# Two node-update ticks behind the last group of each edge stage, instead of ticks ahead of it

## Time and profile before

| | us |
|---|---|
| three runs | 2838.57, 2837.82, 2832.29 (median 2837.82) |
| the profiled execution's own time | 2831.61 |
| span of its trace | 2829.6 |

### The profile page before, as it was taken

How to read it: one execution, slowest core, us unless ns; L and a number is a source line. 1 busy time by engine, 2 the same in 40 slices (tenths; PEclk the granted TensorE clock), 3 DMA queues, 4 the chain that set the end, 5 groups by cost and what they waited for, 6 DMA issues and landing times.

```text
span 2829.6 us, 25622 instructions
## 1 busy us (share of the span) xinstructions
PE 1862.6 (66%) x6464; PEld 875.8 (31%) x6464; DVE 1963.3 (69%) x3488; ACT 1101.4 (39%) x2157; POOL 1862.3 (66%) x1775
## 2 busy tenths in 40 slices
PE   1688778761888567777588856677488868882000
PEld 0333333320344233332244423333244434431000
DVE  4777777743777658999699959999599959972000
ACT  0112121120566435444366625555366636650000
POOL 0777777765775075552677756564577757777776
PEclk7889898975899879999799979999799979995555
DMA  0222222221455434332344434444334434442000
GB/s 15 57 64 64 64 77 64 64 63 44 146 176 176 158 100 136 107 109 95 89 120 128 120 90 146 153 146 149 104 121 125 123 101 140 144 131 63 23 21 20
DMA packets 228924, 285.58 MB, mean 101 GB/s; under 512 B 85309, under 2 KB 100697, under 8 KB 228652
## 3 DMA queue, kind: packets, MB, share of 16 engines
q1 hardware_dynamic: 172332, 257.60, 28.7%
q0 software_dynamic: 56448, 26.34, 5.2%
HBM read 173.01 MB, written 136.00 MB: 109 GB/s over the span
## 4 chain that ended last, share of the span: by engine, by line
DVE 28%; PE 16%; issue 13%; POOL 11%; ACT 6%; DMA 1%; DVEq 0%; SPq 0%; ACTq 0%; POOLq 0%
POOL out_dram L1705 7%; PE bank L1004 6%; DVE mn_total L1400 5%; DVE node_h L1208 5%; POOL mn_ring L447 4%; DVE node_h L1253 2%; PE bank L1756 2%; ACT node_square L1129 2%; DVE node_x L1232 2%; DVE mn_mean L1422 2%; DVE mn_cent L1424 2%; DVE mn_h L1480 2%; PE bank L1008 2%; PE bank L1013 2%; PE bank L998 2%
## 5 line engine op out<-in xcount | busy, mean ns | idle before, releaser
L447 POOL DMA_INDIRECT mn_ring<-slot_rows,addr_i x980 | 1042.4, 1064 | 620.6 <-issue 286.1
L1004 PE MATMUL bank<-node_x,center 128*128 128x512 f32 x492 | 258.4, 640 | 101.9 <-DVE node_h L1208 97.7
L447 POOL DMA_INDIRECT fr_xin<-in_x_dram,src_i x196 | 210.2, 1073 | 125.2 <-issue 125.2
L1008 PE MATMUL bank<-node_square,mean 128*128 128x512 f32 x492 | 263.3, 618 | 35.9 <-ACT node_std L1108 35.9
L447 POOL DMA_INDIRECT found<-node_table,look_i x196 | 210.7, 1075 | 89.1 <-issue 69.1
L1013 PE MATMUL bank<-node_h,wconv 128*128 128x512 f32 x492 | 267.0, 626 | 0.0
L447 POOL DMA_INDIRECT fr_xin<-in_x_dram,dst_i x196 | 204.2, 1042 | 59.7 <-issue 59.7
L595 PE MATMUL bank<-fr_s_lo,fr_s_hi 128*128 128x392 f16 x392 | 149.2, 381 | 138.0 <-DVE fr_d_lo L714 136.7
L1705 POOL DMA_INDIRECT out_dram<-keep,scat_i x196 | 192.6, 983 | 62.4 <-issue 62.4
L1018 PE MATMUL bank<-node_act,wconv 128*128 128x512 f32 x442 | 232.3, 608 | 1.2 <-ACT node_act L1123 1.2
L1123 ACT ACTIVATE node_act<-bank,bias 128x512 f32<-128x512 f32 x246 | 167.9, 682 | 126.1 <-PE bank L1013 125.8
(11 more groups left out here) (320 smaller groups left out, 3857.2 us busy)
## 6 DMA issues: line engine op xcount, KB each, us to landing
mn_ring<-local SPq DMA_DIRECT2D x120, 256.0 KB, 4.3
node_x_in<-in_x_dram SPq DMA_DIRECT2D x98, 256.0 KB, 3.0
out_dram<-node_rows SPq DMA_DIRECT2D x98, 256.0 KB, 3.3
mn_rin<-res SPq DMA_DIRECT2D x96, 256.0 KB, 3.3
local<-node_rows SPq DMA_DIRECT2D x96, 256.0 KB, 2.5
slot_rows<-keep SPq DMA_DIRECT2D x96, 256.0 KB, 2.0
mn_fcol<-f_rows SPq DMA_DIRECT2D x192, 128.0 KB, 4.1
res<-mn_x SPq DMA_DIRECT2D x72, 256.0 KB, 2.5
```

The lines of the kernel that those rows point to most:

```text
L447: return eng.indirect_dma_start(out=dest, out_offset=None, in_=table, in_offset=bass.IndirectOffsetOnAxis(ap=index, axis=0), bounds_check= ...
L1004: pe.matmul(bank[i][:, :], C["center"][:, :], src, start=True, stop=True).then_inc(s["centered"][i], 1)
L1008: pe.matmul(bank[4][:, :], C["mean"][:, :], nd.square[:, i - 1, :], start=True, stop=True) \
```

## The change

The ticks are dealt out anew, and the two that fall to a stage's last group come behind everything that this group has to do. `GAP` gives two ticks to the last group of A to E. `QUIET` leaves none to the groups ahead of it (the test is `g < GROUPS - 3`, so groups 22 and 23). The share of B and D falls from 0.83 to 0.72, since the same 130 ticks must be dealt out.

The diff, with each engine's loop in turn (VectorE, SyncE, TensorE, ScalarE):

```diff
-SHARE = dict(A=1.0, B=0.83, C=1.0, D=0.83, E=1.0, F=1.05)
+SHARE = dict(A=1.0, B=0.72, C=1.0, D=0.72, E=1.0, F=1.05)
+GAP = dict(A=2, B=2, C=2, D=2, E=2, F=0)
+QUIET = dict(A=3, B=3, C=3, D=3, E=3, F=4)
...
-        if g < GROUPS - 2 and (st != "F" or g < GROUPS - 4):
+        if g == GROUPS - 1:
+            due += GAP[st]
+        elif g < GROUPS - QUIET[st]:
             due += SHARE[st]
...
-                    for t in ticks[i][:1]:
-                        head(t)
+                    if g < n - 1:
+                        for t in ticks[i][:1]:
+                            head(t)
...
                     for t in ticks[i]:
-                        if t > ticks[i][0]:
+                        if g == n - 1 or t > ticks[i][0]:
                             head(t)
                         tail(t)
...
-                    for t in ticks[i]:
-                        keep_local(t)
+                    if g < n - 1:
+                        for t in ticks[i]:
+                            keep_local(t)
...
-                    for t in ticks[i]:
-                        tick(t)
+                    if g < n - 1:
+                        for t in ticks[i]:
+                            tick(t)
...
                         store(st, g)
                         if i + 1 < len(order):
                             fill_kv(*order[i + 1])
+                        for t in ticks[i]:
+                            keep_local(t)
+                            tick(t)
...
-                    for t in ticks[i][:1]:
-                        first(t)
+                    if g < n - 1:
+                        for t in ticks[i][:1]:
+                            first(t)
                     if st != "A":
                         product(i, st, g)
+                    if g == n - 1:
+                        back(i, st, g)
                     for t in ticks[i]:
-                        if t > ticks[i][0]:
+                        if g == n - 1 or t > ticks[i][0]:
                             first(t)
                         second(t)
-                    if g == n - 1:
-                        back(i, st, g)
...
-                    for t in ticks[i][:1]:
-                        begin(t)
+                    if g < n - 1:
+                        for t in ticks[i][:1]:
+                            begin(t)
...
-                    for t in ticks[i]:
-                        if t > ticks[i][0]:
-                            begin(t)
-                        rest(t)
                     if st in NORMS and g == n - 1:
                         squares(norm_at(st, g), g)
                         deviation(norm_at(st, g), g)
+                    for t in ticks[i]:
+                        if g == n - 1 or t > ticks[i][0]:
+                            begin(t)
+                        rest(t)
```

## The result

The changed kernel takes **2762.14 us** (median of 4 runs, 2761.4 to 2764.15); the kernel before, in its runs together with a repeat, 2835.07 (4 runs, 2832.29 to 2838.57). The ratio is 0.9743, with a 95% interval of 0.9726 to 0.976. The forecast was 2782, its range 2764 to 2808. The direction and the main mechanism held; the gain was larger than the sum, and the time lies just under the range. The profiled execution took 2762.42 us, its span 2760.5, at a mean granted clock of 0.867 (before: 0.856).

A forecast was written before the change was run, and what follows sets the result against it. No single engine bounds it: VectorE paces steps with ticks, GpSimd is the second limit and sets F's end. Terms summed to -55.4 from 2831.6, giving 2776.2; with 6.2 added, 2782; own range 2770 to 2796, over the cases 2764 to 2808.

The forecast's parts named there:

- C and E: Last steps of stages C and E: group 22 loses its tick, saving 5.2 us in each, -10.4 together.
- The pair: Two ticks behind a stage's last group: 19.9 us, hidden in VectorE's wait for gathers; +3 for overruns at B, C, E.
- R1: Stage ends: TensorE stays at half clock through the pair, 9 us at four or five boundaries; 2822, half 2800; chance 0.09.
- D's start: Start of D: ticks fall on groups 0 and 1, not 1 and 2, so scan 3 comes earlier; -5 us.
- R2: Tickless steps of B, D or E: GpSimd bounds them at 10.9 us, about 18 us in all; 2800; chance 0.08.
- R3: Stage boundaries: next stage's first gather goes behind the pairs, five of 19.9 us in the open; 2877, slower; chance 0.02.
- R5: Stage starts: each gather beside a tick takes twice its 0.99 us, 16 us at five boundaries; 2862, slower; chance 0.01.
- B's term, "-27.4": Steps of B: four ticks fewer at 7.48 us, 29.9, less 1.25 each for groups 22 and 23 at half clock.
- The overrun and the delay at B's start, +1.85: Start of B: +1 us for the pair sticking out, 0.85 for the first two groups' gathers beside a busy VectorE.
- A, "-2.0": End of A: one tick leaves the steps, 2.9 us saved, less 0.9 for a cold step.
- F, "+3.0" and the 0.85: Stage F: two-tick step moved to group 6 delays GpSimd's ring buffers, +3, bounds 0 to +8.5; delayed first gathers, 0.85.
- R4: Cold steps cost nothing, the pair ends early, stage starts run warm: 10 us better, 2772; chance 0.08.

The follow-up runs named there:

- the kernel without quiet steps: Changed kernel with ticks also in groups 22 and 23 of A, C and E, six fewer in B and D; 2756.36 us, ratio 0.9738.
- the run with the double back at 16: Changed kernel with F's step of two ticks moved from group 6 back to group 16; 2768.85 us, ratio 0.9753.

## Why the prediction came out 20 us high

**What held.** The chain of reasons: the gap takes two ticks, and the ticks that leave steps with a full price pay. Windows of the changed kernel, in order: steps 22 and 23 of A; step 6 of B, which has a tick; steps 21 to 23 of B; steps 22 and 23 of C; steps 22 and 23 of E (columns: length, busy of PE, PEld, DVE, ACT, POOL, clock, DMA):

```profile
953.24:962.33 9.09, 6.10 (x24) 3.05 (x24) 5.93 (x10) 3.35 (x7) 0.00 (x0) 0.86 0.23 69
962.33:968.96 6.63, 1.09 (x4) 0.72 (x4) 5.56 (x9) 1.14 (x3) 0.00 (x0) 0.50 0.47 159
...
1079.08:1094.53 15.45, 11.43 (x42) 5.32 (x40) 12.85 (x19) 8.60 (x19) 8.48 (x9) 1.00 0.45 144
...
1280.89:1288.91 8.02, 3.69 (x11) 1.96 (x12) 7.18 (x12) 1.62 (x4) 4.03 (x4) 0.70 0.02 4
1288.91:1296.86 7.95, 6.01 (x14) 2.56 (x13) 7.11 (x11) 1.62 (x4) 0.00 (x0) 0.50 0.40 132
1296.86:1304.82 7.96, 6.02 (x13) 2.34 (x11) 6.86 (x12) 1.62 (x4) 0.00 (x0) 0.50 0.38 132
...
1588.15:1593.32 5.17, 2.25 (x8) 1.45 (x9) 3.16 (x5) 0.69 (x1) 4.26 (x4) 0.81 0.38 110
1593.32:1599.02 5.70, 3.59 (x10) 1.64 (x9) 2.90 (x4) 0.69 (x1) 0.20 (x1) 0.50 0.39 124
...
2207.37:2213.49 6.12, 3.20 (x8) 1.66 (x9) 3.25 (x5) 0.69 (x1) 3.94 (x4) 0.64 0.43 122
2213.49:2219.19 5.70, 3.58 (x10) 1.64 (x9) 2.90 (x4) 0.69 (x1) 0.00 (x0) 0.50 0.33 98
```

*C and E.* Step 22 was forecast at 5.2 and is 5.17 in C; step 23 was to be 0.9 longer than 4.74, for a cold PE (one at half clock), and is 5.70 in both. In E step 22 is 6.12, with the clock at 0.64 already. The repeat of the same kernel had the clock in the same two steps of E:

```profile
2211.73:2216.45 4.72, 1.79 (x8) 1.00 (x9) 3.17 (x6) 0.69 (x1) 3.81 (x4) 1.00 0.36 102
2216.45:2221.20 4.75, 2.22 (x10) 1.18 (x9) 2.90 (x4) 0.69 (x1) 0.66 (x1) 0.85 0.46 137
```

So the cost of a cold PE in a step that VectorE doesn't fill is real, 9.47 against 11.82 us for the two, and whether it is paid varies from run to run.

*The pair* was forecast at 19.9 us, with 8.5 between its ticks, and is 19.3 with 8.45 at the end of E. At the ends of B and D it takes 16.1 and 16.3 us, and at A's end, with local ticks, 17.3 where 22 to 24 were forecast. TensorE's timeline at the end of E, as the earlier trace rows, shows that the clock comes back inside the first tick:

```profile
2223.21 1.91 PE L1013 MATMUL bank<-node_h,wconv 128*128 128x512 f32 x2
2224.92 1.66 PE L1008 MATMUL bank<-node_square,mean 128*128 128x512 f32 x2
...
2226.85 1.02 PE L1013 MATMUL bank<-node_h,wconv 128*128 128x512 f32 x2
```

That refutes R1. *D's start* was to gain 5; its scan 3 comes 54.66 us behind the first gather, before 59.90 (1707.54 - 1647.64). R2 didn't show in B or D: their tickless steps take 7.4 to 8.0 us, not 10.9. R3 is refuted by the first gathers, and by the pair moved to step 23, which is what an unhidden pair looks like. R5: eight gathers beside the pair took 10.66 us at F (2226.27 to 2236.93) and 11.13 to 11.37 at C, D and E; beside an idle VectorE they take 10.10. The prediction got "twice as long" from the lock on the Trainium skill's page "SBUF — State Buffer", section "SBUF: two separate sides". It left out a condition of that page: on VectorE's side the lock is for operations in a two-port mode, and for operations with two SBUF inputs only against a GpSimd operation that reads SBUF. Which of the pair's operations are of these kinds no run here shows. What was measured is 6 to 13%, and R5 is refuted for this mix of operations.

Three of the prediction's signs didn't come as written. The second waits are 3.2 to 5.2 us and not 1 to 3. C and E are shorter by 2.9 and 3.0 and not by 5; the prediction's own terms for them add up to 3.4. And the second L1013 row of the first tick, not of the second, is at 1.02 already.

**The step that failed is the size of B's term, "-27.4".** B fell by 33.6, the forecast with its additions was 25.5: 8.1 us of the 13.7 by which the sum fell short. Three parts:

- *"22 and 23 meet PE at half clock ...: 1.25 us each."* They take 7.95 and 7.96 at a granted clock of 0.50, and 7.95 was the price at 0.79. PE has 6.0 us of work in them, DVE 7: DVE still sets the pace and the slow products hide behind it. This part is 2.5 us. It was wrong to carry the 0.9 over from E, where DVE has only 2.9 and nothing hides them. The same error made D's term 1.3 too small.
- *"15.43"* as the step that goes. On average a step with a tick was dearer than that in the kernel before. Two windows of the kernel before, steps 7 and 9 of B:

```profile
1100.10:1117.51 17.41, 13.66 (x40) 6.62 (x39) 12.94 (x20) 8.81 (x19) 11.37 (x11) 0.81 0.40 127
1132.94:1149.22 16.28, 12.48 (x33) 4.97 (x32) 14.26 (x22) 7.68 (x16) 9.19 (x10) 0.90 0.34 109
```

  DVE is busy for 13 to 14 us of each, and PE works at a granted clock of 0.81 and 0.90. Step 6 of B, ahead of a tickless one, takes 15.45 in the changed kernel, at 1.00. 17.41 + 16.28 - 2 x 15.43 = 2.8 us. This part is luck as far as is known: it stands on one trace of the kernel before, and single steps of 16.4 to 16.5 us at a clock of 0.82 to 0.90 turn up early in B in other kernels of this set too, as steps 4, 6 and 8 of the kernel without quiet steps.
- *The overrun and the delay at B's start, +1.85.* Scan 3 comes 58.3 us behind the first gather, before 59.1: 0.8 us earlier instead of 1.85 later. This part is 2.7 us. The pair delays scan 0 by 5.6 us, but step 0 then takes 6.76 instead of 10.69, and step 1, which took 20.64 us at a clock of 0.78 (first line, the kernel before), takes 16.94 at 0.88 (second, the changed one):

```profile
1009.80:1030.44 20.64, 15.89 (x48) 7.78 (x47) 9.80 (x14) 8.61 (x17) 16.07 (x16) 0.78 0.27 82
1006.95:1023.89 16.94, 14.06 (x48) 6.80 (x47) 9.78 (x15) 8.61 (x17) 12.98 (x14) 0.88 0.31 89
```

*A, "-2.0"*, was -4.6. Its step 23 was priced 0.9 up for a cold PE, and instead falls from 9.09 to 6.63. VectorE waited there for PE in the kernel before:

```profile
967.96 0.69 DVE L1441 SCALAR_TENSOR_TENSOR mn_x<-bank,mn_rin 128x512 f32<-128x512 f32 x1 [2.36 <-PE bank L1772]
```

The same operation in the changed kernel:

```profile
963.52 0.67 DVE L1446 SCALAR_TENSOR_TENSOR mn_x<-bank,mn_rin 128x512 f32<-128x512 f32 x1
```

The wait has gone. A reading, not tried by itself: behind a step with a tick, PE is still at that tick's products when the turn is wanted (4.62 us of PE work in that window, 1.09 in the changed one). The window of before showed 9.09 for a step that follows one with a tick, and I took it for the price of any tickless step; the changed kernel's step 22, which does follow one, takes 9.09 still.

*F, "+3.0" and the 0.85*, was +0.6. Scan 7 was late and group 10 starts 109.3 us behind the first gather (before 107.7), so POOL does lose something: its ring waits in F are 6.7 us in six, the longest 2.1. But the wait of 3.94 at the end goes for it. The bound 0, "all of it eaten by that wait", was the right end, and the run with the double back at 16 confirms that the place of the double decides nothing. Together the misses of A, B, D and F are 15.2 us; C and E came out 0.9 us dearer, C by the later gather of D and E by its step 22, and the parts around the stages 0.6. That leaves 13.7.

**The offset of 6.2.** The median of the three first runs was 6.2 us above the profiled run, and I added it. The changed kernel's profile is 0.3 from its median. The 6.2 was a draw of chance: the untouched part ahead of the main phase took between 697.6 and 706.7 us in the ten profiles that are not from the slow chip, and a median of three carries such a spread. 13.7 + 6.2 = 19.9, the whole error. R4 named cold steps that cost nothing, a pair that ends early and warm stage starts. That held in part: cold steps cost nothing in A, B and D but did in C and E; the pairs at the ends of A, B and D ended early; and B's start ran warmer. Its size (10 us) and its chance (0.08) were too small, and the range's lower end rested on it.

What stays open: why scan 3 of B comes 0.8 us earlier where those of C and E come 1.3 and 0.8 later (C's 0.2 earlier in the repeat), and what varies in the untouched front phase. Neither was tried.

## What to carry to other kernels

Price a piece of filler work in each place by itself: here a tick costs mostly 7 to 8 us where VectorE sets the pace, 5 at the end of a stage that GpSimd feeds, 0.7 to 1.0 in its middle, and about nothing in the wait between two stages, up to the length of that wait. Before putting a price on a half clock, ask which engine ends last in that step; a cost seen in one stage is not to be carried to another with a different pace-setter. And compare kernels by a stretch that only the change can touch (here the main phase) when run-to-run spread elsewhere is as large as the effect.

## What the runs showed of the hardware

- TensorE stayed at its half clock (1.2 GHz, granted 0.50) through B's steps 22 and 23 of the changed kernel, after step 21 with 3.69 us of PE work in 8.02, and each of them itself with 6.0 in 7.95; at the end of E it came back to full within the first tick of the pair: rows of two products of 1.91 us at 2223.21 and 1.02 at 2226.85.
- A half clock costs nothing where VectorE fills the step (7.95 us at 0.50 and at 0.79 in B), and 2.35 us over two steps where it doesn't (E's steps 22 and 23: 9.47 us at 1.00 and 0.85, 11.82 at 0.64 and 0.50, in two runs of one kernel).
- GpSimd's indirect gathers are slowed little by VectorE's work in the pair: eight in 10.10 us beside an idle one, 10.66 to 11.37 beside the pair.
- VectorE in C and E has a step of 11.26 us, just above the 10.4 that eight gathers need; with ticks in about every other step of E, a neighbouring pair of steps took 5.64 and 15.15 us, the same 10.4 on average.
- On one chip every kernel took about 19% longer (3374.86 for 2835). In the changed kernel's profile there VectorE, ScalarE and GpSimd were busy as long as elsewhere within 2%, and TensorE for 2005.4 us instead of 1868.0 at a mean granted clock of 0.803.
